# Eight-wide-head attentions with two tiles in a slot, rope products and row writes partly on GpSimd

## The reference, cut to what matters

```
qh, kh, vh = heads(x @ Wq.T + bq), heads(src @ Wk.T + bk), heads(src @ Wv.T + bv)   # 16 heads of 8
qh, kh = rope(qh), rope(kh)                     # L0a, L2a, L3x; L0x turns its rows instead
scores = einsum('bhqd,bhkd->bhqk', qh, kh) / sqrt(8)
scores = where(mask, scores, lowest)            # causal, banded, by cell or by key
attn = softmax(scores)                          # over 64 keys
x = layernorm(x + einsum('bhqk,bhkd->bhqd', attn, vh).reshape(...) @ Wo.T + bo)
```

## Time and profile before

| | |
|---|---|
| time, median of 3 runs | 4241.38 us (4237.48 to 4247.14) |
| span of the profiled execution | 4192.4 us; the median lies 49.0 us above it, which is launch and end outside the span (the profiled execution's own time has no row) |
| instructions | 135897 |
| busy share: TensorE, VectorE, ScalarE, GpSimd | 86%, 76%, 53%, 41% |
| busy share of TensorE's weight loads | 64% |
| mean granted TensorE clock | 0.929 |

### The profile page before, as it was taken

One profiled execution on the slowest core, in us unless ns is written; L12 is line 12 of the kernel. 1 busy time (PEld: TensorE's weight loads), 2 busy tenths in 40 slices (PEclk: granted clock), 3 DMA queues, 4 the chain that ended last, 5 costly groups with the idle time before them and its releaser, 6 DMA issues. The chain is left out here.

```text
span 4192.4 us, 135897 instructions
## 1 busy us (share of the span) xinstructions
PE 3617.1 (86%) x47928; PEld 2667.3 (64%) x47928; DVE 3194.4 (76%) x7754; ACT 2220.8 (53%) x4048; POOL 1736.0 (41%) x2905
## 2 busy tenths in 40 slices
PE   8996886688799998999996775999999778879986
PEld 6774665455577776777776554777764344557764
DVE  7996994135699887888995177999986678769975
ACT  4665761234444443667882344667873366545553
POOL 4667975633442111122454442332222255435544
PEclk9998995788999999999996887999999899989998
DMA  2002213577200000111001760001112100000001
GB/s 79 28 26 81 64 49 95 149 201 195 79 17 8 1 0 11 43 42 34 17 17 59 226 168 13 14 14 30 33 37 58 39 1 0 0 23 25 23 13 40
DMA packets 306791, 214.81 MB, mean 51 GB/s; under 512 B 51664, under 2 KB 285136, under 8 KB 306384
## 3 DMA queue, kind: packets, MB, share of 16 engines
q1 hardware_dynamic: 246704, 162.31, 13.5%
q0 software_dynamic: 12288, 25.19, 2.0%
q10 hardware_dynamic: 47520, 23.60, 1.9%
HBM read 127.08 MB, written 54.53 MB: 43 GB/s over the span
## 5 line engine op out<-in xcount | busy, mean ns | idle before, releaser
L1533 DVE TENSOR_TENSOR L0f_G<-L0f_SG,L0f_psH 128x512 f32<-128x512 f32 x106 | 73.0, 689 | 208.1 <-remote 99.3
L2477 POOL TENSOR_TENSOR L1a_rs<-L1a_ag,eps 128x1 f32<-128x1 f32 x64 | 13.0, 203 | 400.2 <-DVE L1a_ag L2642 400.2
L703 ACT ACTIVATE L2a_PT<-L2a_psP 128x512 f32<-128x512 f32 x256 | 138.7, 594 | 64.3 <-PE L2a_psP L624 63.9
L755 DVE TENSOR_REDUCE L1x_mx<-L1x_psS 128x16 f32<-128x1024 f32 x128 | 155.9, 1218 | 16.3 <-PE L1x_psS L578 15.6
L755 DVE TENSOR_REDUCE L2a_mx<-L2a_psS 128x16 f32<-128x1024 f32 x128 | 156.3, 1221 | 11.6 <-PE L2a_psS L578 9.5
L703 ACT ACTIVATE L1x_PT<-L1x_psP 128x512 f32<-128x512 f32 x256 | 138.8, 595 | 44.9 <-PE L1x_psP L624 44.3
L774 DVE TENSOR_TENSOR L1x_PR<-L1x_psS,L1x_mx 128x1024 f32<-128x1024 f32 x128 | 156.3, 1221 | 6.3
L774 DVE TENSOR_TENSOR L2a_PR<-L2a_psS,L2a_mx 128x1024 f32<-128x1024 f32 x128 | 155.9, 1218 | 4.2
L1114 POOL DMA_INDIRECT L0f_sorted_x<-X,L0f_IDX x128 | 123.1, 962 | 85.2 <-issue 35.7
L639 PE MATMUL L1x_psB<-VB,L1x_PT 128*64 128x18 f32 x4096 | 141.0, 212 | 0.3 <-DVE L1x_ON L789 0.3
L639 PE MATMUL L2a_psB<-VB,L2a_PT 128*64 128x18 f32 x4096 | 141.0, 212 | 0.3 <-DVE L2a_ON L789 0.3
(11 more groups left out here) (622 smaller groups left out, 11715.2 us busy)
## 6 DMA issues: line engine op xcount, KB each, us to landing
L0f_WB<-in_w12a SPq DMA_DIRECT2D x53, 312.0 KB
L0f_XB<-L0f_sorted_x SPq DMA_DIRECT2D x53, 256.0 KB
L0f_sorted_y<-L0f_YB ACTq DMA_DIRECT2D x53, 256.0 KB
L1m_WB<-in_w12b SPq DMA_DIRECT2D x37, 321.0 KB
L1m_XB<-L1m_sorted_x SPq DMA_DIRECT2D x37, 256.0 KB
L1m_sorted_y<-L1m_YB ACTq DMA_DIRECT2D x37, 256.0 KB
L0x_VS<-in_ctx SPq DMA_DIRECT2D x64, 128.0 KB, 2.8
KB<-L1x_QK SPq DMA_DIRECT2D x256, 32.0 KB, 1.8
```

The costliest lines, as they stand in the source:

```text
L703: nc.scalar.activation(PT[:, A.par, 4 * hb:4 * hb + 4, :], psP[:, hb], ACT.Copy).then_inc(S[done].sem, 1)
L755: nc.vector.tensor_reduce(heads4(mx[:, T.par, :].unsqueeze(2))[:, :, :, 0], psSH, AX, ALU.max).then_inc(S["maxed"].sem, 1)
L1533: nc.vector.tensor_tensor(G[0:f, J % 2, c, :], SG[0:f, c, :], up, ALU.mult).then_inc(S["g_ready"].sem, 1)
L2477: nc.gpsimd.tensor_tensor(rs[:, A.par, 0:1], ag[:, A.par, 1:2], eps[:, 0:1], ALU.add).then_inc(S["var_eps"].sem, 1)
```

## The change

A slot now handles a pair. `Two` numbers pairs, `all_pairs` calls the slots (a loop of two pairs), and the semaphores count pairs. `psS` is used whole: the maximum, the subtraction and the exponential run once over 2048 columns. The transposes of a pair's 16 blocks of probabilities go in four groups of four through the two banks of `psP` (`GROUPS`, `turn_probs`, `copy_probs`), and PT holds both tiles. The steps of `psF` for the pair T+2 (turn, K, Q) and V of T+1 all stand in slot T.

The rope factors: ScalarE copies the raw projection and its partner to `RK` (`raw_parts`, one operation of 512 columns, two of 256 with a bias); then one product of 512 columns with the table, for Q on GpSimd, for K on GpSimd in L2a and on VectorE in L0a and L3x (`products_on_dve`); GpSimd adds the halves as before. Where nothing turns (L1x, L1f, L2x) GpSimd writes the output rows in two operations, elsewhere VectorE still writes them, in L0x in another form. In L1x the keys are no longer multiplied by the key mask (`keymask`, its loads and L855 and L766 are gone; the mask is in `maskk` as before). The raw context for V is loaded a second time, into CV. In L3x the sum on ON (L802) moves to GpSimd. The prologue is 4 pairs instead of 6 tiles.

```diff
-def all_slots(eng, stages):
+def all_pairs(eng, stages):
+    begin, first, ahead = -4, 6, 4
...
-            psO, psOT, psJ = psB[:, 0:HP * VW], psP[:, 0, 0, :], psP[:, 1, 0, :]
-            psSH = psS[:, :, 0:HQ, :]
+            psOT, psJ = psP[:, 0, 0:2, :], psP[:, 1, 0:2, :]
+            o3 = psB[:, 0:2 * HP * VW].rearrange("p (x c) -> p x c", c=VW)
...
+            GROUPS = ((0, 0, 1), (0, 1, 0), (1, 0, 1), (1, 1, 0))
...
+            def rope_product(eng, n, tab):
+
+                parts = RK[:, n].rearrange("p (c s k) -> p c s k", c=2, s=4)
+                return eng.tensor_tensor(parts, parts, rope[:, tab:tab + 2, :].unsqueeze(2).to_broadcast([P, 2, 4, SEQ]), ALU.mult)
...
+                        if not rows_on_dve:
+                            nc.gpsimd.tensor_tensor(RB[:, F.u], RB[:, F.u], mv[:, F.u, :, 0:1].to_broadcast([P, 2, D]), ALU.subtract).then_inc(S["mix"].sem, 1)
+                            made(g, "rstd", F.p + 1)
+                            made(g, "mix", F.p + 1)
+                            pace(g, S)
+                            nc.gpsimd.tensor_tensor(rows_of(F), RB[:, F.u], rs[:, F.u, 1, :].unsqueeze(2).to_broadcast([P, 2, D]), ALU.mult).then_inc(S["out_rows"].sem, 1)
...
+                        if not products_on_dve:
+                            made(g, "o_k", M.p + 1)
+                            rope_product(nc.gpsimd, 0, ck).then_inc(S["gates"].sem, 1)
...
+                def slot(T):
+                    A, N, H = T - 1, T + 2, T - 2 - e
...
+                    if N.ok and not by_rows:
+                        fill_turn(N)
+                    yield
+                    if A.ok:
+                        made(pe, "probs", A.p + 1)
+                        made(pe, "res", A.p - 1 - e)
+                        turn_probs(A, 0)
...
+                        fill_projection(N, src, k, ks, "f_k")
...
+                        turn_probs(A, 1)
+                        made(pe, "pt_a", 4 * A.p + 1)
+                        turn_probs(A, 2)
...
+                        made(pe, "o_k", N.p + 1)
+                        fill_projection(N, XT, q, qs, "f_q")
```

More of the change, by code:

```diff
@@ L665, in slot @@
+                    yield
+                    M = T + 1
+                    if M.ok and not by_rows:
+                        fill_v(M)
                     yield
@@ L883, in _ @@
                 def _(sp):
[L884 removed]
+                    all_pairs(sp, [(s.sync(sp), s.drain) for s in stages])
                     stages[-1].last(sp)
```

726 lines of the change are left out of this document (337 added, 389 removed).

## The result

The changed kernel took 4183.24 us (median of 4 runs, 4166.12 to 4188.95) where the kernel before took 4239.43 beside it: a ratio of 0.9873, 95% interval 0.9831 to 0.9915. Beside each other a second time it was 4153.05 to 4183.77 us, 0.9925, 0.9906 to 0.9944. So it is faster by 0.75 to 1.3%, 31 to 56 us, a small gain but clear of the interval both times. The forecast was 4208, 33 us less; the time lay in the range. That the size came out about right is luck: two errors of opposite sign cancelled, a steady gain three times as large as forecast and a loss where a gain was forecast at the ends of the stages. The rest of this document is about them.

What follows compares the result with a forecast made beforehand. TensorE's work was taken to bound L1f and L2x, VectorE close behind. Terms of -0.88 us a pair times 32 gave -28, edges -5: 33 under the median 4241.4, so 4208 us, range 4155 to 4255.

Steps and rivals of the forecast that it cites:

- TensorE is the bound in L1f and L2x: In L1f and L2x TensorE's own work fills the whole slot, VectorE close behind; period after the change 8.0 to 8.2 us.
- Merging gives 0.08: Every stage: a pair's scores in one group take 1.16 us of TensorE for 1.24, so -0.08 a pair.
- Waits for the exponential -0.2 and for CT -0.75: TensorE's waits that go: for the exponential in L0a and L2a, -0.2 us a pair each; for copy CT in L3x, -0.75.
- The rope copies +0.18: L2a and L3x: the swapped product and two ScalarE copies outlast TensorE's other work, 2.15 against 1.97 us, +0.18 a pair.
- XT's hand-over +0.15: Six stages that turn rows: TensorE waits for ScalarE's copy before K, 0.91 us against 0.27 + 0.50 of work, +0.15 a pair.
- rival 1: TensorE's chain through ScalarE costs more than it frees: slower, 4285 us, deciding from 0.17 us a pair beyond the count; chance 0.19.
- CT between two transpositions +0.64: L3x: copy CT stands between two transpositions with nothing else to cover it, so TensorE waits 0.64 us more a pair.
- L0x: GpSimd's 7.53 becomes the period: L0x: GpSimd no longer waits for VectorE's variance, so its own 7.53 us of work sets the period, -0.5 a pair.
- Rival 3: GpSimd eats the gain in L0x and L0a: 4228 to 4240 us; chance 0.15, shared with a milder ScalarE delay.
- GpSimd in L0a 8.5, under TensorE: L0a: GpSimd's work, own waits and the new 512-column product make 8.5 us a pair, under the 9.3 available.
- Fills and drains -5: Five fills and drains: first pairs start no later, about 1 us less each, bounds -3 to +2, together -5 us.
- rival 2: VectorE was the bound and TensorE only looked full: 12.9 us a pair less, 3830 us, a third of it 4100; chance 0.06.

Runs made afterwards that it cites:

- the new order: Changed kernel with the rows' transposes ahead of the attention rows' transposes, on TensorE and ScalarE alike: 4115.59 us, 0.9841 of the kernel before.
- best_1: Changed kernel with the rows' transposes first and, in L3x, context and rows transposed together with one copy of 512 columns: 4112.19 us, 0.9831 of the kernel before.
- the next change: Rows' transposes put ahead of the attention rows' transposes, against the changed kernel: 4115.59 us, L0a at 9.00 us a pair.

## Why the prediction was right, and where it was wrong

- *TensorE is the bound in L1f and L2x.* Right for the changed kernel, and right in L1x, L2a, L3x and, level with GpSimd, in L0a: 0.43 us more work gave 0.30 to 0.46, 1.2 us more of VectorE's gave 0.00 to 0.02 in L1x, L1f and L2x. For the kernel before it is argued. By the Trainium skill's rule on the most contended engine (Perfetto Trace Analysis, Identifying the Most-Contended Engine) VectorE at 94% would have been first; here the starts of the groups decided, and the runs bear them out. L1f and L2x were to be 8.0 to 8.2 and are 7.80 and 7.83.
- *Merging gives 0.08.* This is the term that failed. It was worked out from the waves of the scores, as if a group's time were its products' own. It is -0.6 in L2x, since each change of tile size on TensorE costs as well, and splitting one group again gave 0.25 to 0.27 of it back. With -0.6 for -0.08 and 0.34 for 0.15 L1f and L2x come to -0.26, where -0.24 and -0.25 were measured.
- *The mask in L1x and L3x -0.10.* Right: 0.97 for 1.06.
- *The OT wait in L1x goes, -0.35.* Right. L1x came to 8.86, forecast near 8.9, but by the same two errors: its other groups got 0.39 shorter and the wait for XT is 0.36.
- *Waits for the exponential -0.2 and for CT -0.75.* About right: the partner's products, 0.53 to the next start before, are 0.43 in L0a and L2a, twice a pair; in L3x the second transposition and the one before it were late by 0.7 together.
- *The rope copies +0.18.* Eight transposes hold Q in L2a and L3x for 1.17 us, 0.87 elsewhere, so 0.30.
- *XT's hand-over +0.15.* It was 0.34, for the copy OT ahead of it on ScalarE and less cover. This is rival 1's mechanism, and 0.19 beyond the count is past the 0.17 from which it was to decide. It did not, for the merging gave more: that the change was not slower is luck as far as this term goes.
- *CT between two transpositions +0.64.* 1.06 - 0.27 = 0.79 us from start to start, and 0.78 of gain when it was taken away with the new order.
- *L0x: GpSimd's 7.53 becomes the period.* 7.42, with GpSimd 98% busy, as it said. But it is only half of it: VectorE's load was to be 6.4 and is 7.2 in 7.4, some 0.5 of that because its row writes take 0.66 on average and not 0.44, so VectorE is level; 1.2 us more of VectorE's gave 1.17, and in best_1 GpSimd 0.73 lighter moved nothing. Rival 3 named such contention and priced it at no L0x gain.
- *GpSimd in L0a 8.5, under TensorE.* Its rows and waits fill 8.9 to 9.0, so it stands level with TensorE. It took everything from the next change; what it took from this one no run shows.
- *Fills and drains -5.* Wrong in sign: +31. "First pairs start no later" was said without working out how many projections now stand ahead of the first scores; first subtractions come 3.4 to 8.8 us later in their stages. The drains were not worked out at all.
- *The span and the median.* The 49 us were one execution against others, in which L0f is the part that varies most, and not launch, which is under 2 us. That did no harm, since the sum was made on differences.
- *Sums.* Besides -0.88 for -0.78, rival 2's periods make 13.2 us a pair less and not 12.9, and rival 3's terms 4227 to 4230 and not 4228 to 4240. Neither bears on the forecast.

Steady gain was forecast at 25 and is 80, edges at 5 of gain and are 31 of loss: -30 by the forecast's terms, -49 in the attentions of the profiles, -31 and -56 by the medians.

## What to carry to other kernels

When TensorE is full, count its groups and not only its products: orders that keep products of one tile size together gain, and a split costs 0.2 to 0.3 us even if nothing waits. Before taking load from an engine, add some to it: if the period does not move, taking load away will not help either. A deeper software pipeline pays for its lead at every start of a stage, and where seven short stages follow each other that took over a third of the gain; and an unchanged stage that varies by 70 us makes periods, not spans, the thing to compare.
